# One more chunk of the Mamba scan multiplied by C through a transpose, and new instruction orders around it

## The reference

```python
x = x + mamba4(reaction_diffusion(x))         # 4 Mamba blocks, d_inner 256, d_state 16
x = x + moe_top2(mlp_with_expert_head(x))     # 8 experts, top 2 of them, d 128, f 512
x = x + causal_attention(pooled_prefix(x))    # 16 heads of 64, keys and values by a rank of 128
x = x + bitlinear_ffn(per_subject_linear(x))  # 8 bit activations, ternary weights
```

```python
dA  = exp(dt[..., None] * A)                    # (b, l, d, s)
dBu = dt[..., None] * Bm[:, :, None, :] * xm[..., None]
h_l = dA_l * h_{l-1} + dBu_l                    # along the 256 positions l
y   = einsum('blds,bls->bld', h, Cm) + xm * D_skip
y   = (y * silu(z)) @ out_w.T
```

## Time and profile before

| what | us |
|---|---|
| median of 3 runs (1281.1 to 1281.54) | 1281.53 |
| the profiled execution, its own time | 1278.62 |
| its span, first to last instruction | 1276.8 |
| TensorE busy | 1219.2 (95%) |
| VectorE busy | 1112.1 (87%) |
| GpSimd busy | 1071.7 (84%) |
| ScalarE busy | 1019.0 (80%) |

### The profile page before, as it was taken

The page is one execution under the profiler, slowest core; times in us unless marked ns, Lnnn a source line. Parts: engine busy times, 40 slices in busy tenths (PEclk is TensorE's granted clock), DMA queues, the critical chain, the costliest instruction groups (busy, mean ns, idle before and its releaser), DMA issues.

```text
span 1276.8 us, 23728 instructions
## 1 busy us (share of the span) xinstructions
PE 1219.2 (95%) x7192; PEld 715.4 (56%) x7193; DVE 1112.1 (87%) x1639; ACT 1019.0 (80%) x2654; POOL 1071.7 (84%) x642
## 2 busy tenths in 40 slices
...
GB/s 185 270 235 173 162 253 162 184 219 158 192 240 141 209 226 135 216 232 142 216 226 121 229 159 211 109 168 60 87 72 53 24 13 25 27 23 18 7 10 14
DMA packets 49594, 178.88 MB, mean 140 GB/s; under 512 B 15672, under 2 KB 33500, under 8 KB 40924
## 3 DMA queue, kind: packets, MB, share of 16 engines
q1 hardware_dynamic: 47180, 172.85, 35.8%
...
## 4 chain that ended last, share of the span: by engine, by line
PE 41%; DVE 36%; ACT 11%; issue 9%; DMA 1%; DVEq 1%; POOL 0%; another core or an unknown queue 0%; ACTq 0%; SPq 0%; POOLq 0%
DVE h L1661 25%; PE banks L347 11%; DVE h L1642 10%; ACT banks L1623 6%; PE banks L524 6%; PE banks L919 4%; PE banks L1024 3%; PE banks L1702 3%; PE banks L535 3%; PE banks L967 3%; PE banks L1448 2%; PE banks L1883 1%; ACT sp L1573 1%; ACT h L1745 1%; PE banks L725 1%
## 5 line engine op out<-in xcount | busy, mean ns | idle before, releaser
L1661 DVE TENSOR_TENSOR_SCAN h<-banks,h 128x1024 f32<-128x1024 f32 x256 | 569.4, 2271 | 1.0 <-ACT banks L1623 0.4
L1667 POOL TENSOR_TENSOR h<-h,Cb 128x1024 f32<-128x1024 f32 (+2 forms) x153 | 522.7, 3443 | 20.6 <-issue 11.4
L1623 ACT ACTIVATE banks<-dt,A_cur 128x255 f32<-128x255 f32 x1024 | 425.8, 462 | 60.9 <-DVE h L1661 56.2
L1702 PE MATMUL banks<-h,ident 128*128 128x512 f32 x912 | 416.9, 597 | 3.2 <-DVE yz L1770 2.3
L1702 PEld LDWEIGHTS banks<-h,ident 128*128 128x128 f32 x912 | 164.9, 190 | 188.8 <-issue 180.8
L1648 POOL TENSOR_TENSOR h<-Bb,u 128x1024 f32<-128x1024 f32 (+1 forms) x63 | 212.9, 3389 | 2.0 <-DVE xs L1562 1.8
L1642 DVE TENSOR_TENSOR h<-Bb,banks 128x1024 f32<-128x1024 f32 (+2 forms) x101 | 183.1, 1859 | 0.9 <-ACT banks L1607 0.7
L960 POOL TENSOR_SCALAR Cb<-Cb,h 128x128 f32<-128x128 f32 x124 | 96.5, 797 | 33.0 <-DVE h L942 32.7
L1448 PE MATMUL banks<-xn,wF 128*128 128x512 f32 x256 | 113.0, 592 | 1.8 <-ACT xn L1440 1.8
L960 POOL TENSOR_SCALAR h<-h 128x128 f32<-128x128 f32 x124 | 92.5, 762 | 16.2 <-DVE h L942 15.8
L1448 PEld LDWEIGHTS banks<-xn,wF 128*128 128x128 f32 x256 | 47.9, 188 | 62.5 <-issue 60.2
...
...
## 6 DMA issues: line engine op xcount, KB each, us to landing
...
```

The costliest lines, as they stand in the source:

```text
L1623: m = e.activation(ps_dA[c % 2][:, g, half, 1:S], dts[q][:, half, i * S + 1:(i + 1) * S], ACT.Exp, scale=A_cur[q][:, s:s + 1])
L1661: e.tensor_tensor_scan(chunk(i, c), ps_dA_flat[c % 2], chunk(i, c), 0.0, ALU.mult, ALU.add).then_inc(sem("scan"), 1)
L1667: e.tensor_tensor(h[i][:, rows(cs), :, :], h[i][:, rows(cs), :, :], both(Cb[i], cs), ALU.mult).then_inc(sem("hC"), len(cs) + (turned_ahead ...
L1702: m = e.matmul(bank(5), ident[:], h_flat[i][:, s * HALVES * S:(s + 1) * HALVES * S], start=(s == GROUP * first_sum(p, i)), stop=(s == NS - 1))
```

## The change

The steady slots turn three chunks of half b (2, 3 and 4) instead of two. GpSimd makes the product of chunk b4, which VectorE made; GpSimd's `C:b3` and TensorE's `sum:b3` go away. The two states of a turned chunk now use banks 4 and 7 in turn. All orders are new, also those of slots 0, 14 and 15 and of attention. The gathers run one slot later (`gather` 3 instead of 4, `comb` 2 instead of 3), with other waits ahead of those of batches 2 and 3, and VectorE waits for the stores of all tiles before its first write of batch 0 to the place where the tiles' outputs lay.

```diff
-POOL_STEADY = ((4, 5, 6), (5, 6, 7))
-TURNED = ((), (2, 4))
-TURN_BANK = {(1, 2): (4, 4), (1, 4): (7, 7)}
+POOL_STEADY = ((4, 5, 6), (4, 5, 6, 7))
+TURNED = ((), (2, 3, 4))
+TURN_BANK = {(1, 2): (4, 7), (1, 3): (4, 7), (1, 4): (4, 7)}
...
-            elif b == 3:
-                if part == 0:
-                    e.wait_ge(sem("x2T"), 4)
-                e.wait_ge(sem(PICK_FOURTH[part][0]), PICK_FOURTH[part][1])
+            elif b == 3 and part == 0:
+                e.wait_ge(sem("x2T"), 4)
...
         def dve_tt(e, b, h):
+            if (b, h) == (0, 6):
+                stored(e, TILES)
...
-            gp=dict(gather=(4, gp_gather), norm=(0, gp_norm)),
+            gp=dict(gather=(3, gp_gather), norm=(0, gp_norm)),
...
-            dve=dict(comb=(3, dve_combine), ...
+            dve=dict(comb=(2, dve_combine), ...
...
-    gp={-2: "gather:0 gather:1 gather:2 gather:3",
+    gp={-2: "",
         -1: "gather:0 gather:1 gather:2 gather:3",
...
-        -1: """k:0 q:0 x2t k:1 at q:1 score:n0 k:2 q:2 score:n1 k:3 q:3 score:n2 S v:0 v:1 turns:n0 score:n3 V:n2 V:n3""",
+        -1: """k:0 q:0 k:1 score:n0 q:1 k:2 score:n1 x2t q:2 at score:n2 q:3 k:3 S v:0 v:1 turns:n0 score:n3 V:n2 V:n3""",
...
-        -1: """comb:l0 k:0 tt:n0 tt:n1 k:2 inv:n0 norm:n0 tt:n2 tt:n3 tt:n4 tt:n5 inv:n1 comb pmax turned:n0""",
+        -1: """k:0 comb tt:n0 tt:n1 tt:n2 inv:n0 tt:n3 k:2 norm:n0 tt:n4 inv:n1 tt:n5 pmax turned:n0""",
...
 ATT_PE = """
-turns:1 score:4 o2 values:0 score:5 pturn values:1 turns:2 score:6 pool fc values:2 q:0 turns:3 score:7 k:0 q:1 fqturn
+turns:1 score:4 values:0 o2 pturn score:5 values:1 pool turns:2 score:6 fc q:0 values:2 turns:3 score:7 k:0 fqturn q:1
...
 ATT_ACT = """
-v:l1 turned:1 yturned:l7 pexp V:2 prob:6 V:3 prob:7 turned:3 yturned:0 prob:8 pturned yturned:1 prob:9 turned:5
+v:l1 turned:1 pexp prob:6 yturned:l7 V:2 turned:3 V:3 prob:7 yturned:0 pturned prob:8 prob:9 yturned:1 turned:5
...
 ATT_DVE = """
-inv:2 tt:6 tt:7 pnorm tt:8 tt:9 turned:2 x3 tt:10 tt:11 inv:3 turned:4 inv:4 tt:12 pool fc tt:13 fq tt:14 turned:6
+inv:2 tt:6 tt:7 pnorm turned:2 tt:8 tt:9 inv:3 x3 comb tt:10 tt:11 pool turned:4 tt:12 fc inv:4 tt:13 fq tt:14
...
 PE_ORDER = """
-sum:l6 back sum:l7 conv:0 conv:1 out z:0 z:1 xproj sum:a0 turnC:b dt:0 dt:1 sum:a1 sum:a2 sum:a3 sum:a4 sum:a5 hT:b20
-sum:a6 hT:b21 sum:a7 +center hT:b40 sum:b0 hT:b41 sum:b1 sum:b3 sum:b5 yT:b20 yT:b21 yT:b40 yT:b41"""
+back sum:l6 sum:l7 conv:0 conv:1 out z:0 z:1 sum:a0 xproj sum:a1 dt:0 dt:1 sum:a2 sum:a3 turnC:b sum:a4 sum:a5 hT:b20
+hT:b21 sum:a6 hT:b30 hT:b31 sum:a7 hT:b40 +center hT:b41 sum:b0 sum:b1 sum:b5 yT:b20 yT:b21 yT:b30 yT:b31 yT:b40
+yT:b41"""
 ACT_ORDER = """
-xn dA:a2 dA:a3 dA:a4 dA:a5 ucopy:b silus xm:0 xm:1 res zs:0 zs:1 exps dA:a6 xd dA:a7 turnC:b dA:b0 sp_abs dA:b1 dA:b2
-sp_exp sp_ln dA:b3 hT:b20 dA:b4 hT:b21 dA:b5 dA:b6 hT:b40 dA:b7 hT:b41 ucopy:n +square +lnv dA:n0 +rstd dA:n1 +scale"""
+xn dA:a2 dA:a3 dA:a4 dA:a5 dA:a6 silus xm:0 xm:1 res ucopy:b zs:0 zs:1 exps dA:a7 xd dA:b0 dA:b1 sp_abs dA:b2 sp_exp
+turnC:b sp_ln dA:b3 dA:b4 hT:b20 hT:b21 dA:b5 hT:b30 dA:b6 hT:b31 dA:b7 hT:b40 hT:b41 ucopy:n +square dA:n0 +lnv
++rstd dA:n1 +scale"""
 DVE_ORDER = """
-mul:a01 mul:a2 mul:a3 mul:a7 scan:a0 scan:a1 scan:a2 scan:a3 gate:l scan:a4 mul:b012 mul:b34 scan:a5 scan:a6 scan:a7
-scan:b0 scan:b1 scan:b2 dt scan:b3 scan:b4 gate:a scan:b5 scan:b6 scan:b7"""
+mul:a01 mul:a2 scan:a0 mul:a3 scan:a1 scan:a2 scan:a3 scan:a4 gate:l mul:a7 scan:a5 scan:a6 mul:b012 scan:a7 scan:b0
+mul:b3 scan:b1 scan:b2 dt scan:b3 scan:b4 scan:b5 gate:a scan:b6 scan:b7"""
 POOL_ORDER = """
-C:l7 mul:a456 mul:b5 C:a012 C:a3 mul:b6 C:a45 C:a67 C:b01 mul:b7 u C:b3 C:b5 C:b6"""
+C:l7 mul:a456 C:a012 C:a3 mul:b4 C:a45 mul:b5 C:a67 mul:b6 C:b01 mul:b7 u C:b5 C:b6"""
 PE_OPEN = """
-lap:1 center lap:2 back lap:3 conv:0 conv:1 z:0 sum:a0 sum:a1 z:1 sum:a2 xproj sum:a3 dt:0 sum:a4 dt:1 sum:a5 sum:a6
-sum:a7 sum:b0 sum:b1 +center sum:b2 sum:b3 sum:b4 sum:b5"""
+lap:1 center lap:2 back lap:3 conv:0 conv:1 sum:a0 sum:a1 z:0 z:1 sum:a2 sum:a3 sum:a4 sum:a5 sum:a6 xproj dt:0 dt:1
+sum:a7 +center sum:b0 sum:b1 sum:b2 sum:b3 sum:b4 sum:b5"""
 POOL_OPEN = """
-mul:a456 C:a012 mul:b6 mul:b7 C:a3 C:a45 C:a67 C:b01 C:b23 C:b4 u C:b5 C:b6"""
+mul:a456 C:a012 mul:b6 C:a3 C:a45 C:a67 mul:b7 C:b01 C:b23 u C:b4 C:b5 C:b6"""
...
 DVE_OPEN = """
-react:1 mul:a0 mul:a12 scan:a0 mul:a3 react:2 scan:a1 scan:a2 scan:a3 mul:a7 scan:a4 scan:a5 react:3 mul:b012 scan:a6
-scan:a7 mul:b345 scan:b0 scan:b1 scan:b2 scan:b3 gate:a scan:b4 scan:b5 dt scan:b6 scan:b7"""
+react:1 mul:a0 mul:a12 scan:a0 mul:a3 react:2 scan:a1 scan:a2 scan:a3 mul:a7 scan:a4 react:3 scan:a5 mul:b012 scan:a6
+scan:a7 scan:b0 scan:b1 mul:b345 scan:b2 scan:b3 scan:b4 gate:a dt scan:b5 scan:b6 scan:b7"""
 PE_NEXT = """
-back conv:0 sum:l6 sum:l7 z:0 conv:1 out sum:a0 sum:a1 sum:a2 z:1 xproj sum:a3 dt:0 sum:a4 dt:1 sum:a5 sum:a6 sum:a7
+sum:l6 back sum:l7 conv:0 out z:0 sum:a0 conv:1 sum:a1 z:1 sum:a2 sum:a3 xproj sum:a4 dt:0 dt:1 sum:a5 sum:a6 sum:a7
...
 DVE_LAST = """
-mul:a0 mul:a1 fin:0 mul:a2 scan:a0 scan:a1 gate:l scan:a2 fin:1 mul:a3 scan:a3 mul:a7 mul:b0 scan:a4 mul:b1 scan:a5
-scan:a6 scan:a7 scan:b0 mul:b2 scan:b1 mul:b3 mul:b4 mul:b5 join:0 scan:b2 scan:b3 gate:a scan:b4 scan:b5 fin:2
+mul:a0 fin:0 mul:a1 mul:a2 scan:a0 scan:a1 gate:l scan:a2 fin:1 mul:a3 mul:a7 scan:a3 mul:b0 mul:b1 scan:a4 scan:a5
+scan:a6 scan:a7 scan:b0 mul:b2 scan:b1 scan:b2 mul:b3 mul:b4 join:0 gate:a scan:b3 scan:b4 mul:b5 scan:b5 fin:2
...
-PICK_THIRD = (("mo_acc", 5), ("mo_acc", 8), ("q_sb", 1), ("ka_sb", 1))
-PICK_FOURTH = (("tt", 1), ("tt", 2), ("tt", 3), ("tt", 5))
+PICK_THIRD = (("mo_acc", 5), ("kv_sb", 2), ("tt", 3), ("tt", 4))
```

More of the change, by code:

```diff
@@ L2563 @@
[L2563 to L2565 removed]
+sum:l6 sum:l7 out up:0 up:1 sum:a0 sum:a1 down:0 sum:a2 sum:a3 down:1 sum:a4 sum:a5 up:2 sum:a6 up:3 sum:a7 down:2
+down:3 lnc:2 sum:b1 sum:b2 lnt:2 logits:3 sum:b3 up:4 logits:0 sum:b5 sum:b6 sum:b7 up:5 outlast ranks:0 lnc:3 down:4
@@ L2566 @@
+down:5 lnt:3 logits:1 up:6 up:7 ranks:1 down:6 down:7 fold:0 logits:2 rows:0 list:0 rows:1 rows:2 fold:1 rows:3
+list:1 ranks:2 total:0 spread:0 fold:2 ahead:0 xt:0 tiling:0 list:2 list:3 fold:3 xt:1 xt:2 xt:3 spin:8"""
 ACT_NEXT = """
-xn dA:a2 dA:a3 silus xm:0 exps dA:a4 shift:0 dA:a5 dA:a6 res dA:a7 ucopy:b dA:b0 silus xm:1 shift:1 zs:0 zs:1 exps xd
-dA:b1 dA:b2 dA:b3 sp_abs sp_exp sp_ln dA:b4 dA:b5 sq:0 dA:b6 rs:0 dA:b7 ucopy:n sc:0 dA:n0 sq:1 rs:1 sc:1 dA:n1"""
+dA:a2 shift:0 xn dA:a3 dA:a4 silus xm:0 exps dA:a5 res ucopy:b dA:a6 dA:a7 silus xm:1 zs:0 zs:1 exps dA:b0 dA:b1 xd
@@ L2569 @@
+dA:b2 sp_abs dA:b3 sp_exp sp_ln dA:b4 dA:b5 sq:0 rs:0 dA:b6 sc:0 dA:b7 shift:1 ucopy:n sq:1 rs:1 sc:1 dA:n0 dA:n1"""
 ACT_LAST = """
-dA:a2 dA:a3 dA:a4 gelus gelu:0 res ucopy:b gelu:1 exps dA:a5 dA:a6 shift:2 dA:a7 rT:0 rT:1 dA:b0 dA:b1 gelus gelu:2
-shift:3 gelu:3 exps dA:b2 rT:2 dA:b3 rT:3 sq:2 ones:0 dA:b4 dA:b5 rs:2 sc:2 dA:b6 dA:b7 gelus gelu:4 gelu:5 sq:3 exps
-rs:3 rT:4 rT:5 gelus gelu:6 gelu:7 rT:6 rT:7 silus rows:0 rows:1 rows:2 fold:0 sums:0 sums:1 fold:1 rows:3 sums:2 columns:0
-fold:2 rexp:0 xt:0 xt:1 xt:2 xt:3 fold:3"""
+dA:a2 shift:2 dA:a3 shift:3 dA:a4 gelus gelu:0 res ucopy:b gelu:1 exps dA:a5 ones:0 dA:a6 dA:a7 rT:0 dA:b0 dA:b1 rT:1
```

55 lines of the change are left out of this document (27 added, 28 removed).

## The result

The changed kernel takes 1273.05 us (median of 14 runs, 1269.06 to 1279.68) beside 1281.53 (14 runs, 1277.24 to 1283.2) for the kernel before: ratio 0.9939, 95% interval 0.9922 to 0.9956. That is 8.5 us less by the medians and 7.8 by the ratio, which goes by the means: inside the range, but little more than half of the 14.4 us forecast. Its profiled execution was one of its slowest, 1278.76 us, so the same kernel was run again (run e1, 1272.8 us profiled) and both profiles are used.

What follows compares the result with a forecast made beforehand. VectorE was taken as the bound, GpSimd close behind. Gains of 10.1 (steady slots), 1.3 (first slot), 1.5 (last two) and 1.5 (attention entry) sum to 14.4 us: median 1267.1 us, range 1260 to 1275.

Steps and rivals of the forecast that it cites:

- Steady slots: Thirteen steady Mamba slots: 48.51 us each falls to 47.73, 10.1 us less in all (bounds 4.6 and 13.8).
- The stall at scan a7: Steady slots: VectorE waits before scan a7 for ScalarE's dA behind two table loads, 0 to 0.5 us, taken as 0.25.
- First slot: First Mamba slot: later gate:a and other new orders gain 1.3 us (0 to 1.64).
- The 1.64 us ahead of gate:a: First Mamba slot: VectorE's wait for the sums before gate:a, 1.64 us, was to go.
- Last two slots: Last two Mamba slots: new orders gain 1.5 us, a third of VectorE's 5.1 us idle (bounds -1.5 to +4).
- Joins: Last two Mamba slots: VectorE's join of two chunks costs 3.37 or 1.19 us; join:0's new place can give either.
- Entry of attention: Before attention slot 0: four gathers instead of eight, comb later; gain 1.5 us (-1 to +4).
- the prediction's two cases: Entry of attention: nothing gained if the copy's remote wait stays; 1.7 us and more if eight gathers in a row caused it.
- Attention slots: Steady attention slots keep their instructions and TensorE has no idle time to give: 0, with -0.3 to +0.3 a slot.
- A: Steady slots: hand-off stalls eat half the gain, a slot of 48.1 us, about 1275 us in all; chance 0.12.
- C: Steady slots: late hT copies on ScalarE hold dA:b6 and VectorE; slower, +5.7 us, 1287 us; chance 0.05.
- D: Steady slots: TensorE falls to its lower clock over 48 transposes a slot; +52 us, 1333 us; chance 0.02.

Runs made afterwards that it cites:

- e3: Kernel before with the steady slots' change alone (third turned chunk, product of b4 on GpSimd, four steady orders): 1274.2 us, ratio 0.9948.
- e7: Changed kernel with chunk 3 of half b still turned, but the product of chunk b4 given back to VectorE: 1283.26 us, ratio 1.0004.
- e4: Kernel before with the attention part alone (gathers and comb one slot later, attention orders): 1276.49 us, ratio 0.9969.
- e5: Changed kernel with ScalarE's ones:0 in slot 15 moved back behind sq:2: 1270.72 us, ratio 0.9906.
- e9: Changed kernel with GpSimd's order of slot 14 alone put back to that of before: 1272.46 us, ratio 0.9929.
- e12: e11 with three loads of slot 15 moved ahead of the load of C in SyncE's queue: 1263.31 us, ratio 0.991.
- e10: Changed kernel with 24 idle matmuls on TensorE in slot 14, ahead of sum:a0: 1273.52 us, ratio 0.9942.
- e2: Changed kernel with the orders of slots 14 and 15 on all four engines put back to those of before: 1268.64 us, ratio 0.9911.
- e11: Changed kernel with GpSimd's order of slot 14 and all four orders of slot 15 put back to those of before: 1267.62 us, ratio 0.9892.

## Why the prediction was right, and where it was wrong

The total fell in the range, but not by its parts: the last two slots came out far beyond their own bounds (-1.5 to +4), and the steady slots and the entry of attention gave about 3 us more than forecast. That these errors went against each other is luck.

- **Steady slots, 10.1 forecast, 10.8 and 11.9 measured** (630.59 less 619.82 and 618.74; 11.9 in e3). The swap works as laid out: GpSimd, priced at 47.69, needs about 47.65, and no scan waits for its product. The stall at scan a7 came as forecast, 0.21 us a slot for the 0.25, though the list of waits is too coarse to show it. VectorE's other work was priced 0.2 too high: with the stall it takes 47.47 and not 47.70. The first profile lists one wait of 0.2 us in the thirteen slots; e1 has one of 1.67 us in slot 1, most of the difference between 10.8 and 11.9. e7 shows that the product alone is the gain.
- **First slot, 1.3 forecast, about 0.5 measured.** The start of slot 0 moves from one execution to the next, so it is best taken inside: from VectorE's scan at 39.37 us to its first product of slot 1 are 49.09 us before, 48.62 in the changed kernel and 48.67 in e1. The 1.64 us ahead of gate:a did not go: it is 1.52. The step reckoned with the later place of gate:a and not with TensorE. TensorE's clock is 0.50 to 0.73 in 76 to 80 us in ten of the eleven profiles with the new orders of slot 0 and 1.00 in those with the old (before, e3, e4), so the sums end later. The eleventh is e5, with the same orders there: 1.00 there, gate:a without a wait, and 47.43 us, 1.7 less than before. So the 1.64 can go, and it was the lower clock that kept it. Why the clock fell in the others was not tried.
- **Last two slots, 1.5 gain forecast, 6.2 to 9.4 loss measured.** This is the step that failed. It took "a third of the idle time" without laying out the orders, as had been done for the steady slot, and put the lag of GpSimd behind the loop at nothing. Three things were there to see. GpSimd leaves the steady slots 2.0 us later against VectorE than before, and the new order puts a product of 2.3 us ahead of C:a01 (e9: taken back, slot 14 is 3.6 us shorter). ones:0 moves from 42 us into slot 15 to 25 us, ahead of the arrival of the table that it reads: ScalarE waits 3.4 us and VectorE 3.3 (gone in e5). And SyncE's queue holds the loads of slot 15 behind GpSimd's last C product; that this costs time is not shown, since e12 took three loads out of its way and slot 15 was no shorter. The rule that a step moved past a queue must be followed there was applied to attention and not here. The lower clock behind such waits, 1.7 us in slot 14 (e10) and 3.0 at the last gate of the first profile, was in no term. By e2 the swap itself costs 1.2 of the loss and the orders the rest; e7, where GpSimd comes out of the loop without the lag, still loses 5.9 us in the two slots: slot 14 gains 1.5, slot 15 loses 7.4.
- **Joins.** Forecast: the new place may give either price, 3.37 or 1.19. Measured 1.50 and 3.35, and 3.31 and 3.35 in e5, where a move on ScalarE shifted them. The prediction took the long one to be the one beside a busy GpSimd, but GpSimd worked beside both. In the kernel before:

```profile
808.10 2.37 POOL L1648 TENSOR_TENSOR h<-Bb,u 128x1024 f32<-128x1024 f32 x1
823.81 3.25 POOL L1667 TENSOR_TENSOR h<-h,Cb 128x1024 f32<-128x1024 f32 x1 [0.35 <-DVE h L1661]
```

The join at 808.18 began 0.08 us behind GpSimd's product and took 3.37. The join at 823.66 began 0.15 us ahead of GpSimd's and took 1.19, and there GpSimd's took 3.25 instead of 2.36. The one that begins second waits for the other; e2 and e11 have the same pairs (1.19 with 3.25, 1.20 with 3.24), and in e11 a join that began 0.47 us behind took 2.98. The Trainium skill (SBUF — State Buffer, "Who interferes with whom") has a VectorE tensor_tensor with two SBUF inputs contend with a GpSimd instruction that reads SBUF; these rows agree.
- **Entry of attention, 1.5 forecast, 2.9 and 3.5 measured;** 3.8 us for the whole part in e4. TensorE's waits of 1.14 and 1.73 us, the latter at 991.41, are gone: it is busy through from 984 to 996. ScalarE's wait of 3.3 us ahead of it, which the profile calls remote, stands in both profiles with the old attention part (before, e3) and in none of the twelve with the new. So it is no chance of one execution, and of the prediction's two cases the one with 1.7 us and more held; whether the gathers or the orders made it was not tried. **Attention slots, 0 forecast:** from the first x3 to the end 242.27, then 242.14 and 243.19.
- **Rivals.** A (hand-offs in the steady slots) and C (hT copies) did not happen. D asked for a lower clock over the transposes: the clock is 1.00 through 126 to 706 us with 48 of them a slot. The rule of the Trainium skill (TensorE: Matmul & The Clock Gate, Part 4: PE-mode transpose) that transposes don't count as busy for the clock made no difference here. The clock did fall, in other stretches: behind gaps in TensorE's work in slots 0, 14 and 15 and the tiles. No rival had that.
